# Causal self attention rewritten: one projection of q, k and v, block-diagonal k, and bank pairs that alternate between natural and turned scores

## What is computed

```python
x = x + L0_attn(layernorm(x))          # x: 64 x 128 x 128
# in L0_attn: 16 heads of 8 features, causal
q = x @ W_dq.T @ W_uq ;  k = x @ W_dkv.T @ W_uk ;  v = x @ W_dkv.T @ W_uv
attn = softmax(causal(q_h @ k_h.T) / sqrt(8))      # per head h, 128 x 128
out = concat_h(attn @ v_h) @ W_o
```

## Time and profile before

| | |
|---|---|
| time, median of 3 runs | 3264.93 us (3261.05 to 3267.30) |
| profiled execution, span | 3260.9 us |
| profiled execution, own time | not recorded apart; the median run lies 4.0 us above this span |
| share of the span busy: PE, PE weight loads, DVE, ACT, POOL | 88%, 73%, 69%, 61%, 55% |
| stage of the change (L249 to L576) | 22 to 599 us of the span |
| its TensorE clock | 1.00 of full speed, the level of 2.4 GHz |

### The profile page before, as it was taken

The page is one execution under the profiler, slowest core; times in us unless marked ns, Lnnn a source line. Parts: engine busy times, 40 slices in busy tenths (PEclk is TensorE's granted clock), DMA queues, the critical chain, the costliest instruction groups (busy, mean ns, idle before and its releaser), DMA issues. The chain is left out here.

```text
span 3260.9 us, 77410 instructions
## 1 busy us (share of the span) xinstructions
PE 2876.7 (88%) x24966; PEld 2373.3 (73%) x24967; DVE 2258.3 (69%) x4939; ACT 1998.5 (61%) x4307; POOL 1809.3 (55%) x3200
## 2 busy tenths in 40 slices
PE   5999999799999999959897799997589999999996
PEld 4666666588888888858786577776367777777775
DVE  4777777467666766545554699997777878787643
ACT  3555555466666666534443466665487777777762
POOL 2223232255666666624555677774576868676752
PEclk9999999799999999979999899998599999999998
DMA  4444444200000000022222100000000000000000
GB/s 131 138 134 122 128 137 134 78 2 6 13 13 13 13 12 13 16 82 76 73 73 67 36 0 0 0 0 1 1 1 5 5 8 5 8 5 8 8 5 10
DMA packets 205069, 128.65 MB, mean 39 GB/s; under 512 B 14256, under 2 KB 197528, under 8 KB 204184
## 3 DMA queue, kind: packets, MB, share of 16 engines
q1 hardware_dynamic: 196632, 108.57, 11.8%
q0 software_dynamic: 8192, 16.79, 1.8%
HBM read 34.82 MB, written 90.51 MB: 38 GB/s over the span
## 5 line engine op out<-in xcount | busy, mean ns | idle before, releaser
L1547 POOL TENSOR_TENSOR a_qk<-a_qkv 128x2048 f32<-128x2048 f32 x64 | 235.3, 3676 | 58.4 <-ACT a_qkv L1522 54.4
L1480 PE MATMUL a_ps_s<-a_qk,w_ident 128*128 128x256 f32 x1024 | 238.3, 387 | 27.5 <-POOL a_qk L1547 27.3
L960 POOL TENSOR_TENSOR x_p<-x_p,x_rz 128x1232 f32<-128x1232 f32 x64 | 143.9, 2248 | 170.8 <-DVE x_rz L1069 170.8
L1480 PEld LDWEIGHTS a_ps_s<-a_qk,w_ident 128*128 128x128 f32 x1024 | 193.2, 194 | 57.3 <-issue 23.0
L199 POOL TENSOR_TENSOR a_four<-stats 128x4 f32<-128x4 f32 (+1 forms) x47 | 9.6, 204 | 384.3 <-DVE stats L529 272.4
L1529 ACT ACTIVATE a_r<-a_o,w_a_rows 128x128 f32<-128x128 f32 x512 | 220.9, 523 | 2.1 <-DVE a_o L1579 2.1
L1338 POOL DMA_INDIRECT f_yg<-f_rows_out,f_index x128 | 122.8, 960 | 176.3 <-DVE f_yo L1418 159.0
L2196 POOL TENSOR_TENSOR x_sq<-x_e 128x1232 f32<-128x1232 f32 x64 | 143.3, 2240 | 129.1 <-DVE x_t_sq L2355 128.9
L512 DVE TENSOR_REDUCE a_nmax<-a_ps_s 128x4 f32<-128x512 f32 x256 | 159.0, 684 | 41.8 <-PE a_ps_s L317 41.8
L421 ACT ACTIVATE a_e<-a_ps_s 128x512 f32<-128x512 f32 x256 | 153.0, 602 | 24.0 <-PE a_ps_s L333 24.0
L1076 DVE TENSOR_REDUCE x_top<-x_ps_s 128x16 f32<-128x1232 f32 x64 | 91.3, 1426 | 109.0 <-PE x_ps_s L700 108.9
(11 more groups left out here) (559 smaller groups left out, 9749.3 us busy)
## 6 DMA issues: line engine op xcount, KB each, us to landing
f_rows_in<-a_zeros SPq DMA_DIRECT2D x31, 1088.0 KB, 5.4
f_rows_out<-a_zeros SPq DMA_DIRECT2D x31, 1088.0 KB, 8.8
f_xin<-f_rows_in SPq DMA_DIRECT2D x135, 64.0 KB
f_rows_out<-f_yo SPq DMA_DIRECT2D x135, 64.0 KB
out<-x SPq DMA_DIRECT2D x16, 256.0 KB
f_raw<-in_late_f SPq DMA_DIRECT2D x2, 1408.0 KB, 6.0
w_ctx<-in_ctx SPq DMA_DIRECT2D x1, 2464.0 KB
f_rows_in<-f_xr,f_where POOLq DMA_INDIRECT x128
```

Of the source, the lines that this page charges most:

```text
L960: nc.gpsimd.tensor_tensor(wide, wide, rz[:, :].unsqueeze(2).broadcast_to([P, HEADS, K]), ALU.mult).then_inc(p_ready, 1)
L1480: ins = nc.tensor.matmul(ps_s[u % 2][:, 0:HEADS * HEADS], c.ident[:, :], qk[:, u % 2, k, :, :], start=k == 0, stop=k == HD - 1)
L1547: nc.gpsimd.tensor_tensor(qk[:, u % 2, :, :, :], qkv[:, u, 0, :, :].unsqueeze(3).broadcast_to(full), qkv[:, u, 1, :, :].unsqueeze(2).broad ...
```

## The change

Each of these is one edit of the diff:

- q and k are projected once each (L420, L421 of the changed kernel), with v in the same bank. The products of scores are plain f32, which takes two instructions each where fp32r took one. The weights are no longer laid out three times over (`latent_weights`).
- k is spread to `k_bd` by POOL (L524): four copies, each with the rows of one head of the strip and zeros in the others. q is used as it is.
- The maxima are bf16 parts in `pad` (128x8 for each head, three filled). PE turns `pad` with one bf16 transpose (L399), DVE multiplies the result into a block-diagonal `m_bd` (L565), and PE adds it to the turned scores with a product of ones (L357, 32 rows, 512 columns bf16, four in a slot).
- The four banks become two pairs. In `half(0)` pair 0 takes natural scores of one batch and pair 1 turned scores of another, interleaved head by head; in `half(1)` the other way round. Maxima and exponentials come two at a time.
- Two heads share 32 rows of `ps_o` in the value product (L390, a window of `v1` shifted by 8 columns), so that `oz` has 256 instead of 512 columns and two transposes (L413) do for four.
- The norm's scalars are worked out for eight batches at a time, in four parts, between the `k_bd` of POOL (`scalars_of`).
- The loop is unrolled by 8 instead of 4, and the lag from the first to the last step is 20 slots instead of 16. `v1` is cleared over 5120 instead of 2048 elements.

```diff
+def scalars_of(c, pool, own, done, s, group, st, second, shift, begun, parts=(0, 1, 2, 3)):
...
+    half, minus_half, minus_one = (c.powers[:, k, 0:group] for k in range(3))
...
-        q, k = (sb(n, [P, UNROLL, GROUP, P], F32R) for n in "qk")
-        q_shift = sb("q_shift", [P, 2, GROUPS, P], F32R)
-        v1 = sb("v1", [P, UNROLL, HEADS, STRIP])
+        q, kT = sb("q", [P, 4, P]), sb("kT", [P, 2, P])
+        k_bd = sb("k_bd", [P, 4, GROUP, P])
+        v1 = sb("v1", [P, RING, HEADS, WIDE])
...
-        AHEAD = 8
-        TURN, PROJECT, SCORE, SHIFT, WEIGH, VALUE, LAST, OUT = (AHEAD + n for n in range(1, 9))
+        AHEAD = 11
+        TURN, PROJECT, SCORE, SHIFT, WEIGH, VALUE, LAST, ADD = (AHEAD + n for n in (1, 2, 4, 5, 6, 7, 8, 9))
+        PAIRS = ((0, 1), (2, 3))
...
+            def half(sl, pair):
+                other = 1 - pair
...
+                    for n, g in enumerate(PAIRS[pair]):
...
+                            pe.wait_ge(exp_done[pair], 2 * (s - 2 + pair) - 1 + n)
+                        masked(ps_s[g], c.mask_q)
...
+                    for n, g in enumerate(PAIRS[other]):
+                        pe.wait_ge(max_done[other], 2 * upto(sl, s + 2 + pair) - 1 + n)
...
+                        masked(ps_s[g], c.mask_k)
+                    pe.wait_ge(shift_ready, s + 1)
+                    for g in PAIRS[other]:
+                        nc.tensor.matmul(ps_s[g][:, :], c.ones16[strip(g), :], m_bd[strip(g), u % 2, :, :], start=False, stop=False)
...
+                        for g in PAIRS[pair]:
+                            nat = nc.tensor.matmul(ps_s[g][:, j * P:j * P + P], q[strip(g), u % 4, :], k_bd[strip(g), u % 4, j, :],
+                                                   start=False, stop=j == GROUP - 1)
...
+                        for g in PAIRS[other]:
+                            turned = nc.tensor.matmul(ps_s[g][:, j * P:j * P + P], k_bd[strip(g), u % 4, j, :], q[strip(g), u % 4, :],
+                                                      start=False, stop=j == GROUP - 1)
...
+                    nc.tensor.matmul(ps_qkv[:, 0:P], c.a0_q[:, :], xT[:, u % 2, :], start=True, stop=True)
+                    nc.tensor.matmul(ps_qkv[:, P:2 * P], c.a0_k[:, :], xT[:, u % 2, :], start=True, stop=True)
+                    nc.tensor.matmul(ps_qkv[:, 2 * P:3 * P], xT[:, u % 2, :], c.a0_v[:, :], start=True, stop=True).then_inc(qkv_ps, 1)
...
+                    nc.gpsimd.tensor_tensor(k_bd[:, u % 4, :, :], kT[:, u % 2, :].unsqueeze(1).broadcast_to([P, GROUP, P]),
+                                            c.block[:, 0:GROUP].unsqueeze(2).broadcast_to([P, GROUP, P]),
+                                            ALU.mult).then_inc(bd_ready, 1)
...
+                    nc.vector.tensor_tensor(m_bd[:, u % 2, :, :], ps_pad.unsqueeze(1).broadcast_to([P, GROUP, P]),
+                                            c.block[:, 0:GROUP].unsqueeze(2).broadcast_to([P, GROUP, P]),
+                                            ALU.mult).then_inc(shift_ready, 1)
```

More of the change, by code:

```diff
@@ L181, in after, with rough_root, newton_terms @@
     def after(ins):
[L182 to L191, removed]
+        n[0] += 1
+        ins.then_inc(own, group)
+        pool.wait_ge(own, steps * begun + n[0] * group)
+    half, minus_half, minus_one = (c.powers[:, k, 0:group] for k in range(3))
+    both, dif, sq, dif2, wide, vpe, rough, square, rate, again = (st[:, k, 0:group] for k in range(10))
+    me, mo, ve, vo = (c.stats[:, bass.ds(s, group), k] for k in (1, 4, 2, 5))
+    mean, rstd, shifts = (t[:, bass.ds(s, group)] for t in (c.mean, c.rstd, c.shift))
+    def rough_root(x):
         after(nc.gpsimd.tensor_tensor(rough, x, minus_half, ALU.pow))
+    def newton_terms(x):
         after(nc.gpsimd.tensor_tensor(square, rough, rough, ALU.mult))
@@ L266, in self_attention @@
         rest = sb("rest", [P, 2, HEADS])
[L267 to L271, removed]
+        pad = sb("pad", [P, 2, HEADS, HD], BF16)
+        m_bd = sb("m_bd", [P, 2, GROUP, P], BF16)
+        e = sb("e", [P, 2, GROUPS, GROUP, P])
+        oz = sb("oz", [P, 2, P])
+        rz = sb("rz", [P, 2, GROUPS, HALF])
         o = sb("o", [P, 2, D])
@@ L357, in slot @@
+                    for j in range(GROUP):
+                        two, low = divmod(j, HALF)
+                        for g in range(GROUPS):
+                            ins = nc.tensor.matmul(ps_o[strip(g), two * P:two * P + P],
+                                                   v1[:, u, GROUP * g + j, HD - HD * low:WIDE - HD * low], e[:, u % 2, g, j, :],
+                                                   start=low == 0, stop=low == HALF - 1)
+                    ins.then_inc(o_ps, 1)
                 if at := sl.step(SHIFT):
@@ new lines, in slot @@
+                if at := sl.step(LAST):
+                    s, u = at
+                    pe.wait_ge(oT_ready, s + 1)
+                    wait(pe, x_done, s)
+                    nc.tensor.matmul(ps_y[:, 0:P], oT[:, :], c.w["a0_o"][:, :], start=True, stop=True).then_inc(y_ps, 1)
+                if at := sl.step(TURN):
+                    s, u = at
+                    pe.wait_ge(xn_ready, s + 1)
+                    wait(pe, xT_ready, s)
+                    wait(pe, oz_ready, s + TURN - VALUE + 1)
+                    nc.tensor.transpose(ps_x, xn[:, u % 2, :], c.ident[:, :]).then_inc(xT_ps, 1)
@@ L433, in slot @@
+                wait(act, o_ps, s - 1)
+                for g in PAIRS[pair]:
+                    nc.scalar.activation(e[:, u % 2, g, :, :], ps_s[g][:, :].rearrange("p (t q) -> p t q", t=GROUP),
+                                         ACT.Exp, scale=scale).then_inc(exp_done[pair], 1)
+            def slot(sl):
+                weighed = sl.step(WEIGH)
+                if weighed:
+                    exponential(weighed, 1)
                 if at := sl.step(VALUE):
@@ L550, in slot @@
                     for n in range(2):
[L551 removed]
+                        part = pad[:, u % 2, :, n]
+                        nc.vector.tensor_copy(part, left).then_inc(own, 1)
                         dve.wait_ge(own, 4 * s + 2 * n + 1)
[L553 to L554 removed]
+                        nc.vector.tensor_tensor(rest[:, n, :], left, part, ALU.subtract).then_inc(own, 1)
```

428 lines of the change are left out of this document (192 added, 236 removed).

## The result

| kernel | time, median (range) | ratio to before, 95% interval | stage of the change ends at |
|---|---|---|---|
| before, same chip | 3262.99 us (3253.23 to 3267.30) | 1 | 599.8 us |
| changed | 3174.8 us (3169.94 to 3178.33) | 0.9732 [0.9714, 0.9751] | 513.5 us |

The time is 88 us shorter; 3173 was predicted. The end of the stage is the start of ACT's first instruction for the next one. It came 86.3 us earlier, and the program behind it took 2658.0 us of the span where it took 2661.1. That code is the same in both, and in the fourteen profiled executions here it took between 2652 and 2673 us, so its 3 us are scatter and the gain lies in the stage of the change. (For the same reason the end of the stage tells small effects better than the time does.) The agreement is closer than the reasoning deserves: two misses of opposite sign nearly cancel, as the rows show.

The account below looks back on a forecast made before the run. PE's own work was taken as the bound, 7.66 of 8.59 us a slot; terms of 6.94 plus 0.20 waits gave 7.14. Over 64 slots 92.8 saved, 1 added: 3264.9 - 92 = 3173 us, range 3148 to 3230.

Parts of the forecast that it names:

- y, x, o: On PE, output product, transpose of the input and transpose of the output: 0.33, 0.20 and 0.17 us a slot.
- scores and ones: On PE, 64 f32 score instructions in two blocks, 2.03 us a slot, and four new products of ones, 0.43.
- waits: PE's waiting in a slot: 0.2 us left, where 0.93 was lost before.
- what one more instruction costs in a block on strips: PE's score blocks, priced from two old blocks: 0.026 us for each instruction and 0.18 for the block.
- Unchanged: PE's output product and the transposes of input and output keep their old prices: 0.33, 0.20 and 0.17 us.
- C: Theory tried in the experiments: POOL's k_bd holds DVE's split of the maxima, and so the next maxima and mask.
- together +1: Start and end of the stage, with larger clearing, fewer weight copies and longer lag: 1 us added, between -1 and +5.
- POOL: nobody waits for `k_bd`: POOL's 64 k_bd products of about 1.2 us stay hidden, two slots ahead of their use.
- Within 0.3 us: Sign in the profile: DVE's maxima start within 0.3 us of the scores' end.
- The weight loads in the open: Rival in PE's score blocks: loads not hidden under their strip's products, halfway a 9.3 us slot and 3312 us; chance 0.05.
- DVE sets the pace: Rival: DVE's stretch closes a ring of 7.5 to 8.0 us, 3215 us at 7.8; chance 0.22 shared with the ring.
- The pairs don't loosen the ring: Rival: waits stay 0.5 to 0.9 us a slot, slots 7.5 to 8.3, 3196 to 3247 us; 0.22 shared with DVE.

Follow-up runs that it names:

- e7: Changed kernel with loop written out and k_bd after DVE's split, plus q and k_bd rounded to fp32r (one instruction per score product): 3096.6 us, slot 5.82.
- e6: Changed kernel with loop written out and k_bd after DVE's split, plus the four products of ones done twice, adding zeros: 3187.4 us, slot 7.24.
- e3: Changed kernel with its loop written out and POOL's k_bd waiting until DVE has split the maxima: 3155.4 us, ratio to before 0.9680, slot 6.81.
- e2: Changed kernel, loop kept, with POOL's k_bd waiting until DVE has split the maxima: 3169.6 us, ratio to before 0.9718, slot 6.81 with four long.
- e8: Changed kernel, loop kept, with POOL working out k_bd twice in a row: 3230.5 us, slots of 7.66 to 7.82, four long.
- e5: Changed kernel, loop written out, k_bd after DVE's split, each half's natural products all before its turned ones: 3215.5 us, slot 7.70.
- e4: Kernel before the change with its loop unrolled by 8 instead of 4, nothing else: 3277.1 us, ratio to before 1.0052, slot 8.59 with four long.

## Why the prediction came out right, and where it was wrong

**The slot: 7.14 predicted, 6.97 measured.** Its terms, from start to start in the timeline above:

| term | predicted | measured |
|---|---|---|
| y, x, o | 0.33 + 0.20 + 0.17 | 0.22 + 0.11 + 0.12 |
| qkv | 0.67 | 0.67 |
| `pad` and `oz` | 0.13 + 0.22 | 0.06 + 0.27 |
| values | 1.02 | 1.02 |
| scores and ones | 2.03 + 0.43 | 2.41 |
| masks | 1.74 | 1.92 |
| waits | 0.20 | 0.17 |

- The step "what one more instruction costs in a block on strips", 0.026, was right in the sum that it led to and carried the largest term. In the rows four instructions, two natural and two turned, start every 0.11 us (294.57, 294.68, 294.79). e7 halved the instructions and gave 0.98 back, 0.031 for each: the price of one is higher and the fixed 0.18 of a block lower than was read from the old rows. e6 confirmed the ones to the hundredth.
- "Unchanged" was wrong for y, x and o, by 0.25 in sum. Their prices in the earlier trace rows held a share of their neighbours: y and o followed a block on strips, x stood before one, and y and x carried about 0.1, o 0.05, for the change between strips and full rows. In their new places they don't, and the masks before each block do: 0.53 for two, where two others take 0.43. That is why the masks are 0.18 dearer. The numbers fit this reading; no run tested it alone.
- The waits were sized right and put down to nothing in particular. They are C. DVE's stretch was forecast at 3.6 us, though its own terms add up to 3.25 if the split counts five operations of seven; it takes 3.44 in e3 (291.89 to 295.33), and 4.12 in the changed kernel (292.11 to 296.23), where `k_bd` holds the split.

**The missed step.** The forecast counted the unrolling by 8 only as light slots and cleared memory ("together +1"). What it left out is the return of the loop: 19 us in four of them. It is the mirror of the slot's error, 64 x 0.17 = 11 us too dear. The sum 64 x (8.59 - 6.97) = 104, less 19, makes 85; the last 16 slots, written out behind the loop, are 6.81 to 6.87 and bring 2 more. The stage fell by 86.3, and start and end were worth +1 or less, as said. The trace of before could not show the price, since its returns cost nothing; a bound from both sides was called for, and it was not given.

**"POOL: nobody waits for `k_bd`".** True of PE by its semaphores, and `k_bd` took 1.05 us where 1.16 was worked out. The step failed by asking only who waits: an operation under cover on POOL held an instruction of DVE that reads the same memory. e2 and e8 show it in both directions.

**The profile's signs.** The stage takes 490 us (485 said), SP's bytes go out at 156 GB/s as worked out, PE's wait for ACT fell to 2.1 (on the side of the weight loads, where it was 78.4). Two of the signs named for a wrong forecast appeared in a weak form: the weight loads waited for `nmax` in 60 of 64 slots, at a price of 0.17 us a slot, and the clock fell at three returns. Of DVE's two pairs of maxima one starts with the end of the scores; the other starts at 296.23 where the scores ended at 295.55, since DVE was at its statistics. "Within 0.3 us" held for one of two. The first mask starts at 36.03, before 45.

**The rivals.** *The weight loads in the open* would make a step 0.19 to 0.29 us. It is 0.11, with eight loads in each strip, the price of the product alone. The Trainium skill's rule in "TensorE: Matmul & The Clock Gate", Part 3, that a load overlaps only with products of other rows, gave 0.21 a step and a slot of 8.8; the trace disagrees. The same part also says that a load into the background weight buffer may be pulled ahead, which the prediction left out; the step of 0.11 would fit that statement. Even e5, where fewer strips share the block, adds only 0.45 a half. *DVE sets the pace* was the nearer danger: another 0.7 us held in DVE's stretch makes it true, as e8 shows at 7.7 to 7.8. *The pairs don't loosen the ring*: fallen, the 78.4 us in which the loads of masks waited for exponentials became 2.1.

## What to carry to other kernels

A number that agrees does not show that the reasoning does: compare slot by slot, and look for slots that differ from their neighbours. When a change makes a loop's body larger, price the return apart (here nothing with 4 slots in the body, 4 to 7 us with 8), and try it on the old kernel alone. An operation hidden on POOL is free only if DVE has no small operations beside it that read SBUF with two inputs or cast; place it beside reductions from PSUM instead. And a product's price from start to start holds for its neighbours too: read it at two places before calling it unchanged.

## What the runs showed of the hardware

- A return of the loop with 8 slots cost PE 2.5 to 2.8 us without work (up to 3.4 in e4) and, where the clock fell with it (granted 0.58 in the next 3.6 us), another 1.4. PE's branch took 3.85 to 4.15 us, and the instruction queue brought 54 packets of 16 KB in 340 us. The loop of 4 slots of 204 matmuls and loads returned at no cost, with a branch of 0.21 us and no packet in that queue.
- DVE's cast of 128x16 took 0.93 us instead of 0.20, and its subtraction of two SBUF operands 0.95, when started beside a POOL product of 1.05 us. Beside such products in e2, maxima and reciprocals from PSUM (0.69 and 0.25 us) and the statistics of one SBUF input (0.28) kept their times.
- f32 products on four interleaved strips start four instructions in 0.11 us with a weight load for each; where the block's ends ran on two strips (e5) the same work, with its ones, took 1.65 us instead of 1.20.
- The same four-strip block in fp32r, with half the instructions, took 0.71 instead of 1.20 us with its ones: at 128 columns an instruction in fp32r costs what one of the two of f32 does.
